# A two-layer attention kernel on one Trainium2 core: 53 terms of the causal mask as constant rows of the score stacks

## What is computed

```python
q = x @ W_dq.T @ W_uq.T                                   # 16 heads of 8
attn = jnp.einsum('bhql,bkl->bhqk', q_lat, c_kv) / sqrt(hs)
causal = jnp.tril(jnp.ones((T, T), dtype=bool))
attn = jnp.where(causal[None, None], attn, -jnp.inf)
attn = jax.nn.softmax(attn, axis=-1)
```

## Time and profile before

| | |
|---|---|
| Time, median of 3 runs | 670.15 us (667.65 to 670.68) |
| The profiled execution, its own time | 668.22 us |
| Its span from the first to the last instruction | 666.3 us |
| TensorE busy | 591.4 us (89%) |
| VectorE busy | 389.0 us (58%) |
| ScalarE busy | 362.3 us (54%) |
| GpSimd busy | 168.1 us (25%) |
| DMA: packets, bytes, mean rate | 28869, 35.59 MB, 53 GB/s |

### The profile page before, as it was taken

How to read it: one execution, slowest core, us unless ns; L and a number is a source line. 1 busy time by engine, 2 the same in 40 slices (tenths; PEclk the granted TensorE clock), 3 DMA queues, 4 the chain that set the end, 5 groups by cost and what they waited for, 6 DMA issues and landing times.

```text
span 666.3 us, 16657 instructions
## 1 busy us (share of the span) xinstructions
PE 591.4 (89%) x6886; PEld 381.6 (57%) x6886; DVE 389.0 (58%) x969; ACT 362.3 (54%) x742; POOL 168.1 (25%) x314
## 2 busy tenths in 40 slices
PE   4386899989999999999999999999999998895874
PEld 2133465558665765666665766586667664553653
DVE  1466657685758485657658575857674755124331
ACT  3200456674667466746765576656675667572320
POOL 4364101231213312223214230412133103112111
PEclk9999999999999999999999999999999999997875
DMA  3574100530043104410252014210430000000000
GB/s 78 142 169 94 34 8 8 123 100 8 16 115 88 40 9 110 99 40 3 68 129 57 4 41 109 66 41 12 118 88 25 9 3 16 25 1 3 1 18 16
DMA packets 28869, 35.59 MB, mean 53 GB/s; under 512 B 3931, under 2 KB 25242, under 8 KB 27642
## 3 DMA queue, kind: packets, MB, share of 16 engines
q1 hardware_dynamic: 28794, 34.53, 20.5%
HBM read 24.46 MB, written 9.96 MB: 52 GB/s over the span
## 4 chain that ended last, share of the span: by engine, by line
PE 54%; DVE 11%; issue 6%; ACT 4%; POOL 3%; POOLq 0%; DVEq 0%
PE ps_v L819 7%; PE ps_s L800 6%; PE ps_e L785 5%; PE ps_a L747 4%; PE ps_a L735 3%; DVE cand L1292 3%; PE ps_c L884 2%; PE ps_e L782 2%; PE ps_s L803 2%; PE ps_c L866 2%; PE ps_a L710 2%; PE ps_c L960 2%; DVE stats L1220 1%; DVE hid L1276 1%; PE ps_c L853 1%
## 5 line engine op out<-in xcount | busy, mean ns | idle before, releaser
L1292 DVE TENSOR_REDUCE cand<-ps_s 128x4 f32<-128x512 f32 (+1 forms) x320 | 213.7, 686 | 68.8 <-PE ps_s L803 48.5
L1096 ACT ACTIVATE prob<-ps_e 128x512 f32<-128x512 f32 x320 | 188.5, 598 | 95.3 <-PE ps_e L785 91.4
L800 PE MATMUL ps_s<-kst,qst 72*128 72x128 bf16 (+1 forms) x1024 | 131.0, 243 | 11.8 <-DVE cand L1292 10.6
L785 PE MATMUL ps_e<-qst,kst 75*128 75x384 bf16 (+3 forms) x512 | 121.5, 299 | 0.0
L800 PEld LDWEIGHTS ps_s<-kst,qst 72*128 72x128 bf16 x1024 | 75.1, 102 | 75.6 <-DVE cand L1292 43.4
L819 PE MATMUL ps_v<-prob,vaug 128*32 128x512 f32 (+3 forms) x1024 | 88.6, 441 | 0.0
L782 PE MATMUL ps_e<-identb,negmask 128*128 128x256 bf16 (+1 forms) x320 | 80.7, 252 | 7.0 <-ACT prob L1096 6.7
L785 PEld LDWEIGHTS ps_e<-qst,kst 75*128 75x128 bf16 x512 | 50.2, 98 | 17.6 <-issue 0.3
L803 PE MATMUL ps_s<-negmask,identb 128*128 128x512 bf16 x128 | 52.3, 409 | 0.0
L782 PEld LDWEIGHTS ps_e<-identb,negmask 128*128 128x128 bf16 x320 | 31.2, 98 | 18.6 <-ACT prob L1096 14.3
L819 PEld LDWEIGHTS ps_v<-prob,vaug 128*32 128x32 f32 x1024 | 23.5, 108 | 30.0 <-issue 25.2
(11 more groups left out here) (314 smaller groups left out, 926.1 us busy)
## 6 DMA issues: line engine op xcount, KB each, us to landing
qst<-q_scratch SPq DMA_DIRECT2D x48, 192.0 KB
kst<-k_scratch SPq DMA_DIRECT2D x16, 576.0 KB
q_scratch<-qparts SPq DMA_DIRECT2D x24, 128.0 KB, 2.3
k_scratch<-kparts SPq DMA_DIRECT2D x24, 128.0 KB, 2.3
xn<-in_L_attn_x_dram SPq DMA_DIRECT2D x8, 256.0 KB, 3.2
x_res<-in_L_attn_x_dram SPq DMA_DIRECT2D x8, 256.0 KB, 2.8
out_dram<-second SPq DMA_DIRECT2D x7, 256.0 KB, 2.4
max_scratch<-mrow SPq DMA_DIRECT2D x16, 96.0 KB, 1.8
```

Of the source, the lines that this page charges most:

```text
L785: last = mm(ps_e[:, bank, at:at + TOK - P * j], k[0:SROWS, hd, tok(j)], q[0:SROWS, hd, P * j:TOK], start=False, stop=True, skip_group_chec ...
L800: last = mm(ps_s[:, bank, w * n:w * (n + 1)], q[0:PAIRS, hd, tok(i)], k[0:PAIRS, hd, keys[0]:keys[1]], start=(n == 0), stop=True, skip_gro ...
L1096: af(prob[:, u, :], ps_e[:, u % 2, :], ACT.Exp).then_inc(S["e_emptied"], 1)
L1292: vec.tensor_reduce(cand[:, i, h0:h0 + FILLS * (len(hds) - 1) + 1:FILLS, S_SLOT[u]], ps_s[:, u % 2, :].rearrange("p (a c) -> p a c", a=len ...
```

## The change

Row 75 + r of a q stack holds row r of the identity, and row 75 + r of a k stack holds row r of the mask, for r from 0 to 52 (`MROWS` = 53), repeated over tokens and heads. They are made once, on GpSimd in the memory of `prob`, and copied by four DMAs into the four stacks. A score product of a diagonal tile then runs over all 128 rows and so adds the first 53 mask terms itself; the mask products keep the columns 53 to 127 of each tile. In the E pass a score product is split where the diagonal tile ends: 128 columns over 128 rows, and the rest over 75 rows as a product of its own. In the S pass the diagonal units run over 128 rows; since rows 72 to 74 of `qst` must be zero there, each stack load gets a fifth DMA that writes zeros to them, and the maximum rows are written over these later.

```diff
-STACK_DMAS, WRITE_DMAS = 4, 6
+STACK_DMAS, WRITE_DMAS = 5, 6
+MROWS = 128 - SROWS
...
+        zeros_bf = sb("zeros_bf", [PARTS, TOK], BF16)
+        q_pad, k_pad = (prob[0:MROWS, 0, 256 * n:256 * n + 256].bitcast(BF16).rearrange("p (i c) -> p i c", c=P) for n in range(2))
...
                 sp.dma_start(kst[p][PAIRS:SROWS, :, :], bcast(ones_bf[:, :], 1, HEADS)).then_inc(S["ones_loaded"], 16)
+            sp.wait_ge(S["pad_ready"], 2)
+            sp.wait_ge(S["zeros_ready"], 1)
+            for p in range(2):
+                for st, pad in ((qst[p], q_pad), (kst[p], k_pad)):
+                    sp.dma_start(st[SROWS:P, :, :], bcast(pad.rearrange("p i c -> p (i c)"), 1, HEADS)).then_inc(S[f"pads_loaded{p}"], 16)
...
+                sp.dma_start(qst[b.parity][PAIRS:SROWS, heads, :], bcast(zeros_bf[:, :], 1, HALF_HEADS)).then_inc(loaded, 16)
                 sp.dma_start(kst[b.parity][0:PAIRS, heads, :].rearrange("p h q -> p (h q)"), bcast(k_rows, 1, PARTS)).then_inc(loaded, 16)
...
+            g.memset(zeros_bf[:, :], 0.0).then_inc(S["zeros_ready"], 1)
+            g.tensor_copy(q_pad, bcast(identb[0:MROWS, :], 1, NT)).then_inc(S["pad_ready"], 1)
+            g.tensor_copy(k_pad, bcast(negmask[0:MROWS, :], 1, NT)).then_inc(S["pad_ready"], 1)
...
                 if u < 4:
-                    diag = ps_e[:, bank, 0:P].rearrange("p (a c) -> p a c", a=1)
+                    diag = ps_e[:, bank, MROWS:P].rearrange("p (a c) -> p a c", a=1)
                 else:
                     step = 384 if u < 8 else 256
-                    diag = ps_e[:, bank, :].rearrange("p (a c) -> p a c", c=P)[:, 0:step // P + 1:step // P, :]
-                mm(diag, negmask[:, :], bcast(identb[:, :], 1, len(todo)), start=True, stop=False, skip_group_check=True)
+                    diag = ps_e[:, bank, :].rearrange("p (a c) -> p a c", c=P)[:, 0:step // P + 1:step // P, MROWS:P]
+                mm(diag, negmask[:, :], bcast(identb[:, MROWS:P], 1, len(todo)), start=True, stop=False, skip_group_check=True)
                 for hh, j, at in todo:
                     hd = head_of(grp, hh)
-                    last = mm(ps_e[:, bank, at:at + TOK - P * j], k[0:SROWS, hd, tok(j)], q[0:SROWS, hd, P * j:TOK],
+                    last = mm(ps_e[:, bank, at:at + P], k[:, hd, tok(j)], q[:, hd, tok(j)],
                               start=False, stop=True, skip_group_check=True)
+                    if j < NT - 1:
+                        last = mm(ps_e[:, bank, at + P:at + TOK - P * j], k[0:SROWS, hd, tok(j)], q[0:SROWS, hd, P * (j + 1):TOK],
+                                  start=False, stop=True, skip_group_check=True)
...
+                if b.c < 2 and grp == 0 and u == 0:
+                    pe.wait_ge(S[f"pads_loaded{b.parity}"], 32)
+                rows = P if u < NT else PAIRS
...
-                    last = mm(ps_s[:, bank, w * n:w * (n + 1)], q[0:PAIRS, hd, tok(i)], k[0:PAIRS, hd, keys[0]:keys[1]],
+                    last = mm(ps_s[:, bank, w * n:w * (n + 1)], q[0:rows, hd, tok(i)], k[0:rows, hd, keys[0]:keys[1]],
                               start=(n == 0), stop=True, skip_group_check=True)
                 if u < NT:
-                    last = mm(ps_s[:, bank, :].rearrange("p (a c) -> p a c", a=GH), identb[:, :], bcast(negmask[:, :], 1, GH),
+                    last = mm(ps_s[:, bank, :].rearrange("p (a c) -> p a c", a=GH)[:, :, MROWS:P], identb[:, :],
+                              bcast(negmask[:, MROWS:P], 1, GH),
                               start=False, stop=True, skip_group_check=True)
```

More of the change, by code:

```diff
@@ L318, in two_layers @@
         k_scratch = nc.dram_tensor("k_scratch", (2, PARTS, HD, HEADS, TOK), BF16).ap()
-        names = """const_ready mask_step loaded ones_ready ones_loaded prep_pe prep_out prep_out2 prep_sign small_zeroed b2_ready
+        names = """pad_ready pads_loaded0 pads_loaded1 zeros_ready const_ready mask_step loaded ones_ready ones_loaded prep_pe prep_out prep_out2 prep_sign small_zeroed b2_ready
         first_loaded cent_ss_ready cent_rn_ready masks_ready
```

## The result

The changed kernel takes 803.14 us (median of 4 runs, 799.97 to 804.67) against 670.41 us for the kernel before (4 runs, 667.65 to 672.86). The ratio is 1.199 with a 95% interval of 1.194 to 1.204. The forecast was 819 us, slower, within 790 to 940. The profiled execution took 802.34 us with a span of 799.7.

A forecast was written before the change was run, and what follows sets the result against it. The prediction took PE's columns to bound the main loop and the load of x the start. It summed 668.2 us - 10 us for shorter mask products + 161 us of pad delay = 819 us, range 790 to 940.

The forecast's parts named there:

- One engine for 53 rows: Pad DMAs at the start: 53 is prime, so one DMA engine gets all 3392 packets, 166 us.
- the rule on divisors: DMA transfers: the engines used are the largest number up to 16 that divides the rows.
- (a): Pad DMAs: spread over all engines, the gain wins; 665 us, 661 or 674 at its variants; chance 8%.
- (b): DMA queue: later transfers pass the pads, so only PE's new wait counts; 763 us; chance 4%.
- The packet: Pad DMAs: a 1 KB packet costs a lone engine 49 ns, with ends 43 and 115.
- Rival (c): Pad DMAs: a lone engine is as slow as three were, 115 ns a packet, 1043 us; from 82 ns on 7%.
- The delay: Start: x of sequence 1 comes behind the pads, at about 188 instead of 26.8 us; 161 us late.
- The gain: Score passes: shorter mask products save some 22 us gross on PE, 10 us at the end, ends 4 and 14.
- The steps of the S pass: S pass on PE: 128 mask products go from 512 to 300 columns, 11.7 us less.
- the 2.9 us of the 128-column form: E pass: 128 mask products go from 128 to 75 columns; 2.9 us if time follows columns, half counted.
- Rival (d): Mask products: they don't get shorter because a weight load or the banks pace the unit; 829 us; chance 10%.
- The small additions: GpSimd's three more tiles, 1.5 us, and a fifth DMA per stack load, 1.0 us, both hidden: 0.

The follow-up runs named there:

- experiment 1: Changed kernel with each pad DMA cut into one of 48 rows and one of 5, in the same place: 682.57 us, ratio 1.019 to the kernel before.
- experiment 2: Changed kernel with 51 constant rows instead of 53, everything else as it is: 708.94 us, run once.
- experiment 7: Changed kernel with the uncut pads of parity 1 issued behind the stack loads of sequence 1, those of parity 0 left in place: 788.12 us, run once.
- experiment 4: Changed kernel with pads cut in 48 + 5 rows and the E pass put back to its old products, so only S is changed: 689.63 us, run once.
- experiment 5: Changed kernel with pads cut in 48 + 5 rows and the S pass put back to its old products, so only E is changed: 687.80 us, run once.
- experiment 8: Changed kernel with cut pads moved: parity 0's before the small weights, parity 1's behind sequence 1's stack loads, ones rows behind its x: 665.98 us, ratio 0.996 to before.
- experiment 6: Changed kernel with each uncut pad DMA split by heads into two of 53 rows x 8 heads, in the same place: 804.68 us, run once.
- experiment 9: Changed kernel without pad transfers; VectorE copies the constants into partitions 64 to 127 of all four stacks: 657.42 us, ratio 0.982 to the kernel before.
- experiment 3: Changed kernel with all score and mask products as before; pads and zeros are loaded and waited for but unused: 817.86 us, run once.

## Why the prediction was right, step by step

**One engine for 53 rows: right, and shown.** The DMA share of 6.7% is one engine, and experiments 1 and 2 change little but the engines' number (the bytes stay the same in 1 and fall by 4% in 2) and remove 121 and 97 of the 144 us. The rows of the kernel before proved it less than the prediction says: a share of 76.9% can be 12 engines at work all the time or 16 some of it. It was the rule on divisors that chose, and the runs bore it out. Rivals (a) and (b) are out: no transfer passed the pads, and experiment 7, where half of them are in front, has half of the delay.

**The packet: 43.4 ns, not 49.** This is the term that was mis-sized. 3392 packets took 147 us and not 166. I chose the 49 ns of the 128-row writes as the nearest row and kept 43 as the lower end; the lower end was the value. Rival (c), a slow lone engine, is refuted. That the ones rows' three engines held each other up isn't borne out either: in experiment 2 three engines took 45 ns a packet. Why the ones rows show 115 is open.

**The delay: 143.9 us, not 161.** The route was right in its sum and wrong in one link. I had x queued on the engine behind the pads; in fact SP was held in issuing, and x was not issued until the pads were done (165.38). The sum is the same, since either way x comes behind all 3392 packets; that much was luck, as the held issue was in no row that I had read. One sign of the prediction failed with it: no pad DMA took over 100 us from issue to landing, since SP was never more than one DMA ahead, which makes it some 74 us (twice 36.8, an estimate from SP's rows). The forecast stretch of some 160 us from 18 us on is one of 147 us, at 24 GB/s instead of 21, and the first unit stands at 181.8 instead of 199. With 43.4 ns a packet the prediction's own route gives 18 + 147 + 3 - 27, some 142 us. From DVE's first work on sequence 1 to the first unit it is 11.1 us as before, and nothing behind had slack, as forecast.

**The gain: 10.5 us, against 10.** The steps of the S pass hold: L821 is followed after 0.13 us (326.99 to 327.12) and L794 with 150 columns after 0.07, as forecast. In the E pass I counted half of the 2.9 us of the 128-column form; with 75 columns it is followed after 0.03 us (327.12 to 327.15), so its time follows the columns and the whole counts in PE's work. The split units cost some 0.3 us a repetition beyond their columns (experiments 4 and 5), where the prediction had nothing. The 10 us that it worked out from the Trainium skill's 81 ns a pair ("TensorE: Matmul & The Clock Gate", "Back-to-back issue gap") don't appear: a pair of 128 columns takes 55 to 58 ns here. That PE's work falls by 20.0 us (591.4 to 571.4) and the time by only half of it was in the sum; experiments 4 and 5 show where: of 1.46 us in each pass, 0.88 and 0.50 arrive. That the total came within half a microsecond of the forecast is partly luck. Five repetitions give 5 x 1.39 = 7 us in every kernel with 53 rows and both passes changed; the rest lies in the stages at both ends, where the clock differs between executions, so that what follows the first unit is shorter than before by 8.3 us in experiment 8, 8.4 in 6, 10.5 in the changed kernel, 11.4 in 9 and 12.0 in 1.

**Rival (d), mask products that don't get shorter,** is refuted by the repetitions of 69.46 us. The small additions cost nothing at the end, as assumed: experiment 3 has the repetitions of before with the fifth DMA in each stack load.

Sum with measured terms: 668.2 - 10.5 + 143.9 = 801.6, against 802.3 for the profiled execution.

## What to carry to other kernels

Before a DMA is written, factor the number of its rows: 53 rows went to one engine at 24 GB/s, 51 to three, 48 and 5 as two DMAs to all, for a difference of 121 us here. Ask next whether the transfer must be a DMA at all, and what stands behind it in its queue: an engine that would have waited made the same constants in 9 us that cost nothing, while the well-cut transfer still took 23 us out of the start, and 8 us when it was issued elsewhere. And a gain measured in one engine's busy time (20 us) is not the gain in time (10.5 us); the two passes kept 60% and 34% of theirs.

## What the runs showed of the hardware that was not expected

- SP can be held in issuing a DMA: 35 to 37 us for each one while one engine works through 848 packets, and this with about 870 packets outstanding in one case and 440 in another (experiment 6). So a slow DMA stops not only later transfers on its engine, but all that SP has yet to issue: the load of x was issued at 165.38 where it was at 23.54.
- Packets of 1 KB from on-chip memory to on-chip memory cost 43.4 ns on a lone engine (24 GB/s), 45 ns with three, and 110 ns with all engines at work (132 GB/s together). Sixteen engines were 5.6 times as fast as one, not 16 times. Why was not tried.
- PE's clock doesn't rise at the same distance from the start of the work. For good it is up 34 us after the first unit in the changed kernel (215.3), 51 us after it in experiment 6 (232.6), which has the same products and the same start, and 57 us after it in experiment 3 (238.3). Before the last low stretch ended, PE was busy 5.92 of 6.8 us at 1.2 GHz in experiment 6 and 9.68 of 10.2 in experiment 3. In the kernel before the mask products, in PE's rows in order of time, show it 34 us after the first unit:

```profile
70.94 0.63 PE L803 MATMUL ps_s<-negmask,identb 128*128 128x512 bf16 x1
...
71.67 0.38 PE L803 MATMUL ps_s<-negmask,identb 128*128 128x512 bf16 x1
```

  What decides between them is open. The granted clock that the profile prints for the kernel before reads 1.00 from 37.87 to 71.5, where these products take 0.63 us as they do at 1.2 GHz; so at the start of this trace it is the durations that tell the level.
